# Second attention of a four-stage transformer kernel: the first scores run three slots ahead, the sixteen shifts are turned and sent together, and the visits to TensorE's whole array are regrouped

## The reference

```
x = LN(x + attention0(x))     # 16 heads of 8, rotary embedding
x = LN(x + ffn0(x))           # ternary weights, gelu, inner LN, 512 wide
x = LN(x + attention1(x))     # below
x = LN(x + ffn1(x))           # gated silu, 384 wide
```

```
h = LN(x) * ln_g + ln_b
qk, v = split(h @ W_kv)                   # one projection serves as query and as key
scores = qk[h] @ qk[h].T                  # 16 heads, 256 x 256
a1 = softmax(scores, axis=-1)
a1 = W_x mixed over heads                 # 16 x 16
o1 = a1 @ v ;  return o1 @ W_out
```

## Time and profile before

| What | Value |
|---|---|
| median of three runs | 1552.67 us |
| the profiled execution's own time | 1553.82 us |
| its span, first to last instruction | 1551.6 us |
| TensorE busy (matmuls) | 1467.2 us, 95% of the span |
| TensorE weight loads | 1145.0 us |
| VectorE busy | 1187.8 us, 77% |
| ScalarE busy | 1051.0 us, 68% |
| GpSimd busy | 966.2 us, 62% |
| mean granted TensorE clock | 0.975 of full speed |

### The profile page before, as it was taken

How to read it: one execution, slowest core, us unless ns; L and a number is a source line. 1 busy time by engine, 2 the same in 40 slices (tenths; PEclk the granted TensorE clock), 3 DMA queues, 4 the chain that set the end, 5 groups by cost and what they waited for, 6 DMA issues and landing times. The chain is left out here.

```text
span 1551.6 us, 55296 instructions
## 1 busy us (share of the span) xinstructions
PE 1467.2 (95%) x17642; PEld 1145.0 (74%) x17642; DVE 1187.8 (77%) x3338; ACT 1051.0 (68%) x2581; POOL 966.2 (62%) x1160
## 2 busy tenths in 40 slices
PE   5999999999999799979999999999999999998998
PEld 3444555554554399959888888888888888997997
DVE  4777888888888478887878888788878887864666
ACT  2466777777778788856767777777777777774332
POOL 4555565655654067777778877887788777852222
PEclk8799999999999999979999999999999999999999
DMA  5344544454454100122222222222222222200111
GB/s 144 101 131 119 136 128 134 127 136 132 131 136 117 45 32 30 43 87 76 78 72 78 80 76 76 79 80 77 73 81 80 78 70 82 77 23 28 64 64 51
DMA packets 174124, 133.93 MB, mean 86 GB/s; under 512 B 13787, under 2 KB 145126, under 8 KB 174054
## 3 DMA queue, kind: packets, MB, share of 16 engines
q1 hardware_dynamic: 172944, 132.37, 29.4%
q10 hardware_dynamic: 1110, 0.66, 0.1%
HBM read 64.82 MB, written 55.05 MB: 77 GB/s over the span
## 5 line engine op out<-in xcount | busy, mean ns | idle before, releaser
L934 DVE TENSOR_REDUCE shifts<-bank 128x2 bf16<-128x512 f32 x1024 | 684.4, 688 | 169.7 <-PE bank L1086 166.0
L879 ACT ACTIVATE probs<-bank 128x512 f32<-128x512 f32 x1024 | 573.6, 594 | 139.6 <-PE bank L1072 138.2
L1034 PE MATMUL bank<-values,probs 64*128 64x129 f32 x8192 | 579.6, 277 | 3.8 <-DVE o_even L901 0.7
L1034 PEld LDWEIGHTS bank<-values,probs 64*128 64x128 f32 x8192 | 527.1, 188 | 30.6 <-issue 10.8
L1086 PE MATMUL bank<-stack 48*128 48x256 bf16 x2048 | 367.8, 277 | 38.8 <-DMA stack<-score_parts 20.6
L1072 PE MATMUL bank<-stack 49*128 49x256 bf16 x2048 | 376.4, 274 | 8.5 <-ACT probs L879 3.1
L680 POOL TENSOR_TENSOR values<-mix,v_in 128x1024 f32<-128x1024 f32 x128 | 302.0, 2361 | 0.0
L1072 PEld LDWEIGHTS bank<-stack 49*128 49x128 bf16 x2048 | 166.1, 95 | 140.8 <-ACT probs L879 90.2
L689 POOL TENSOR_TENSOR o_odd<-o_odd,scaled 128x256 f32<-128x256 f32 x224 | 163.3, 729 | 161.4 <-ACT scaled L803 161.1
L1086 PEld LDWEIGHTS bank<-stack 48*128 48x128 bf16 x2048 | 156.4, 96 | 61.8 <-DVE shifts L934 24.4
L803 ACT ACTIVATE scaled<-bank,recips 128x128 f32<-128x128 f32 x448 | 137.6, 357 | 88.7 <-DVE recips L928 88.7
(11 more groups left out here) (165 smaller groups left out, 2179.4 us busy)
## 6 DMA issues: line engine op xcount, KB each, us to landing
stack<-score_parts SPq DMA_DIRECT2D x64, 512.0 KB, 4.0
stack<-score_parts SPq DMA_DIRECT2D x256, 96.0 KB
score_parts<-parts SPq DMA_DIRECT2D x256, 64.0 KB, 2.1
score_parts<-parts SPq DMA_DIRECT2D x128, 96.0 KB, 2.3
score_parts<-parts SPq DMA_DIRECT2D x64, 192.0 KB, 2.3
x_in_f<-x_all SPq DMA_DIRECT2D x64, 128.0 KB, 2.0
score_parts<-parts SPq DMA_DIRECT2D x64, 128.0 KB, 2.3
x_in<-in_L_attn_x SPq DMA_DIRECT2D x32, 128.0 KB, 4.3
```

Source lines behind the costliest of these rows:

```text
L879: act.activation(probs[:, s % RING, :, :].rearrange("p t n -> p (t n)"), s2[s % 2][:, :], ACT.Exp, scale=scale).then_inc(exp_done, 1)
L934: dve.tensor_reduce(shifts[:, :, hf, col], s1_bank(s)[:, :].rearrange("p (t n) -> p t n", t=TILES), op=ALU.max, axis=AX.X, negate=True).th ...
L1034: return pe.matmul(pv_bank(h)[:, q * (D + 1):(q + 1) * (D + 1)], probs[rows, h % RING, t, q * P:(q + 1) * P], values[b.odd][rows, t, h, :] ...
```

## The change

- **Lead.** First scores run `LEAD = 3` slots further ahead: slot s holds index s+3 of batch i+1, and slots 13 to 15 hold indices 0 to 2 of batch i+2. `first_score` and `max_of_head` keep `h = s ^ 1`, now of the shifted index. Step -1 does the first three indices besides its own.
- **Shifts.** All sixteen maxima of a batch go into one buffer (two buffers in turn), are turned by two transposes at slot 13, copied once, and sent by one DMA. SyncE issues it between the two halves of `stack_in`.
- **Visits.** There are three: slot 8 (transposes of `x` and `o`), slot 11 (projection of `q`, now for batch i+3, and output projection), slot 13 (projection of `v`, then all shifts).
- **Copies and splits.** ScalarE takes `exact` at slot 12, part 0 at slot 13 (from `exact` in SBUF instead of PSUM) and part 1 at slot 15. GpSimd's two subtractions move from slots 2 and 5 to 13 and 15. The two normalisations, both at slot 15 before, stand at slot 15 and slot 0.
- **Waits.** `parts_out` waits until the stack of batch i+1 has been read (before: batch i). `take_qk` waits for `y_ready` of batch i-1.

The core of the diff:

```diff
+LEAD = 3
-        self.shifts1 = 2 if first else 1
-        self.shifts0 = 10 if first else 9
+        self.shifts1 = 2 if first else None
+        self.shifts0 = 10 if first else 13
-        self.xt, self.xt_ahead = (6, 4) if first else (13, 3)
-        self.q, self.q_ahead = (14, 4) if first else (1, 2)
+        self.xt, self.xt_ahead = (6, 4) if first else (8, 3)
+        self.q, self.q_ahead = (14, 4) if first else (11, 3)
-        self.ot = 10 if first else 9
+        self.ot = 10 if first else 8
-        self.split = 3 if first else 2
+        self.split = 3
...
+    def first_scores_at(i, on, s):
+
+        if first:
+            return [(i.plus(1), s)] if on(1) else []
+        lead_in = isinstance(i.half, int) and i.number() < 0
+        if s < HEADS - LEAD:
+            scores = [(i.plus(1), s + LEAD)] if on(1) else []
+        else:
+            scores = [(i.plus(2), s + LEAD - HEADS)] if on(2) and not (lead_in and i.number() == -2) else []
+        if lead_in and i.number() == -1 and s == 0:
+            scores = [(i.plus(1), k) for k in range(LEAD)] + scores
+        return scores
...
+        def all_shift_rows_in(b):
+
+            wait_apart(sp, shift_rows_ready, b.number() + 1)
+            rows = core.stack[b.odd][SHIFT_ROW:SHIFT_ROW + TILE_ROWS + 1:TILE_ROWS, 1, :, :]
+            sp.dma_start(rows.rearrange("q r n -> q (r n)"), shift_rows[:, :]).then_inc(shifted[0], 16)
...
-                wait_apart(sp, stacked[0], times(i, 0, n) * (16 * reads))
-                wait_apart(sp, stacked[1], times(i, 0, n) * (16 * reads))
+                read = times(i, 0 if first else 1, n) * (16 * reads)
+                wait_apart(sp, stacked[0], read)
+                wait_apart(sp, stacked[1], read)
...
                 stack_in(i.plus(2), i, on, 0)
+            if not first and on(1):
+                all_shift_rows_in(i.plus(1))
+            if on(2):
                 stack_in(i.plus(2), i, on, 1)
...
-                if s == 2 and on(slots.split):
+                if s == 13 and on(slots.split):
                     split(i.plus(slots.split))
-                if s == 5 and on(slots.split):
+                if s == 15 and on(slots.split):
                     last_part(i.plus(slots.split))
...
+            wait(act, y_ready, times(b, -4, n))
             wait(act, rest_ready, times(b, -1, n))
-            act.activation(exact[:, 0, :], m1[:, 0:TOK], ACT.Copy).then_inc(qk_taken, 1)
...
+            act.activation(exact[:, 0, :], m1[:, TOK:2 * TOK], ACT.Copy).then_inc(qk_taken, 1)
+
+        def first_part(b):
+
+            wait(act, parts_written, times(b, -2, n) * (16 * writes))
+            act.wait_ge(qk_taken, times(b, 0, n))
+            act.activation(parts[b.odd][:, 0, 0, :], exact[:, 0, :], ACT.Copy).then_inc(part0_ready, 1)
...
                 if not first and s == slots.norm and on(-1):
-                    norm(i.plus(-1))
+                    norm(i.plus(-1), (0,))
+                if not first and s == (slots.norm + 1) % HEADS and on(-2):
+                    norm(i.plus(-2), (1,))
...
+        def all_shifts_turned(b):
+
+            pe.wait_ge(max_done, (b.number() + 1) * HEADS)
+            for t in range(TILES):
+                to = SHIFTS_AT + t * P
+                last = pe.transpose(m0[:, :].bitcast(BF16)[0:P, to:to + P], shifts[b.odd][:, t, :], core.ident_bf[:, :])
             last.then_inc(shifts_in_psum, 1)
...
                 if h == BESIDE:
-                    pe.wait_ge(shift_rows_ready, (b.number() + 1) * 2)
-                    pe.wait_ge(part0_ready, times(b, 2, n))
+                    pe.wait_ge(shift_rows_ready, b.number() + 1)
                     pe.wait_ge(v_taken, times(b, 1, n))
...
+            *before, ahead = first_scores_at(i, on, s) or [None]
+
             def score(row_tile, t):
                 if s % 2 == row_tile:
                     if on(0):
                         second_score(i, s, t)
-                elif on(1):
-                    first_score(i.plus(1), s, t)
...
+                elif ahead:
+                    first_score(*ahead, t)
```

More of the change, by code:

```diff
@@ L654, in step @@
                     parts_out(b)
-            if on(1):
+            if first and on(1):
                 shift_rows_in(i.plus(1), 0)
@@ L851, in step @@
                     wait(act, values_ready, times(i, 1, n) * (2 * TILES))
-                    act.activation(v_in[:, :, :].rearrange("p t d -> p (t d)"), m0[:, TOK:2 * TOK], ACT.Copy).then_inc(v_taken, 1)
+                    act.activation(v_in[:, :, :].rearrange("p t d -> p (t d)"), m0[:, 0:TOK], ACT.Copy).then_inc(v_taken, 1)
+                if not first and s == 15 and on(slots.q_ahead):
+                    second_part(i.plus(slots.q_ahead))
                 if s == 13 and first and on(0):
@@ L857, in step @@
                     act.activation(o_t[:, :], m1[:, 0:TOK], ACT.Copy).then_inc(ot_ready, 1)
-                if s == slots.shifts0 and on(1):
+                if first and s == slots.shifts0 and on(1):
                     shift_rows_out(i.plus(1), 0)
+                if not first and s == slots.shifts0 and on(1):
+                    all_shift_rows_out(i.plus(1))
                 if s == slots.xt + (1 if first else 0) and on(slots.xt_ahead):
@@ L986, in _ @@
         if not first:
-            dve.memset(shifts[:, :, :, half_heads:P], 0.0).then_inc(ones_ready, 1)
+            for k in range(2):
+                dve.memset(shifts[k][:, :, HEADS:P], 0.0).then_inc(ones_ready, 1)
         for v in values:
@@ L1213, in others_of_second @@
                     pe.wait_ge(pv_taken, (i.number() * half_heads + (BESIDE // 2 + 1)) * TILES)
-                shifts_turned(i.plus(1), 0)
+            if s == slots.xt and on(3):
+                b = i.plus(3)
+                pe.wait_ge(x_loaded[b.odd], (b.half + 1) * 16)
+                for t in range(TILES):
+                    last = pe.transpose(m1[:, TOK + t * P:TOK + (t + 1) * P], x_in[b.odd][:, t, :], core.ident[:, :])
+                last.then_inc(xt_in_psum, 1)
             if s == slots.ot and on(-1):
                 pe.wait_ge(o_ready, times(i, -1, n))
-                wait(pe, y_ready, times(i, -2, n))
-                if on(0):
-                    pe.wait_ge(pv_taken, (i.number() * half_heads + (BESIDE // 2 + 1)) * TILES)
                 for t in range(TILES):
@@ L1222, in others_of_second @@
                 last.then_inc(ot_in_psum, 1)
+            if s == slots.q and (on(slots.q_ahead) or on(-1)):
+                wait(pe, xt_ready, times(i, slots.q_ahead, n))
+                wait(pe, ot_ready, times(i, -1, n))
+            if s == slots.q and on(slots.q_ahead):
+                b = i.plus(slots.q_ahead)
+                pe.matmul(m1[:, TOK:2 * TOK], core.w1_qk[:, :], x_t[b.odd][:, :], start=True, stop=True).then_inc(qk_in_psum, 1)
             if s == slots.out and on(-1):
-                pe.wait_ge(ot_ready, times(i, -1, n))
-                if on(1):
-                    pe.wait_ge(shift_rows_ready, i.plus(1).number() * 2 + 1)
                 for t in range(TILES):
@@ L1239, in others_of_second @@
                 for t in range(TILES):
-                    last = pe.matmul(m0[:, TOK + t * P:TOK + (t + 1) * P], x_t[b.odd][:, t * P:(t + 1) * P],
+                    last = pe.matmul(m0[:, t * P:(t + 1) * P], x_t[b.odd][:, t * P:(t + 1) * P],
                                      core.w1_kv[:, 1, :], start=True, stop=True)
                 last.then_inc(v_in_psum, 1)
-            if s == slots.xt and on(3):
-                b = i.plus(3)
-                pe.wait_ge(x_loaded[b.odd], (b.half + 1) * 16)
-                for t in range(TILES):
-                    last = pe.transpose(m1[:, t * P:(t + 1) * P], x_in[b.odd][:, t, :], core.ident[:, :])
-                last.then_inc(xt_in_psum, 1)
+            if s == slots.shifts0 and on(1):
+                all_shifts_turned(i.plus(1))
         def step(i, on):
```

78 lines of the change are left out of this document (41 added, 37 removed).

## The result

The change made the kernel slower: 1569.44 us, the median of 5 runs (1562.86 to 1575.3), against 1552.67 before. The ratio is 1.0102 with a 95% interval of 1.0074 to 1.0131. The forecast was 1546. The profiled execution has a span of 1567.3 us, 15.7 more than before.

A forecast was written before the change was run, and what follows sets the result against it. TensorE's own instruction list was taken to set the pace, 22.16 us a step; +0.8 - 0.32 - 0.67 = -0.19 a step over thirty steps, -6 us, with about 1 gained at the start, gave 1546 us, range 1528 to 1572.

The forecast's parts named there:

- The start gains about 1: At the start, about 1 us gained: second batch's stack earlier, against three more maxima ahead of the first step.
- tile term: In each steady step, both scores of a slot on one row tile cost +0.8 us; bounds nothing to +3.6.
- balance: Slots 11 and 12: the tiles get equal work, without a gap after a visit, so +0.
- Rival 1: TensorE's row tiles wait for each other: 1577 us (chance 0.09, partly) or 1631 us (0.05, wholly).
- three visits: Three visits instead of four, two shift transposes instead of four: 3.13 us against 3.45, so -0.32 a step.
- the stalls: Short stalls in a step fall from 0.87 to 0.2 us as copies and normalisation are spread: -0.67.
- rival 3: Spreading does nothing; stalls come from VectorE's maxima and reciprocals and stay at 0.87: +0.48 a step, 1567 us, chance 0.10.
- the shifts come in time: From slot 13's transposes to slot 0, the shift rows' road likely takes 2.5 of 3.5 us: cost nothing, at worst +0.5.
- Rival 2: Shifts come late: slot 13's turning or slot 0's scores wait 0.6 more than allowed; +0.41 a step, 1565 us, chance 0.14.
- stack and parts: Stack halves are needed three slots (3.3 us) earlier, parts are ready before their step begins: cost 0.
- the prediction's own mark: Period of L1206's loads should be 21.97 us; the prediction is wrong if above 22.3 or below 21.5.

The follow-up runs named there:

- e1: The new kernel with a slot's first scores back on the row tile that the second scores leave free (head s instead of s ^ 1): 1538.48 us.
- e6: The new kernel with the upper products, those of the free tile, ahead of the lower ones in even slots: 1565.11 us.
- e7: The new kernel with a lead of four slots instead of three: 1565.80 us.
- e5: The new kernel with the edits of e1 and e4 together and nothing else: 1531.97 us.
- e4: The new kernel with lead-in steps -3 and -2 split at slot 11 and SyncE's next-stage loads issued ahead of step 30's: 1564.24 us.
- e3: The new kernel with each upper product one place later in the slot's list: 1588.31 us.
- e2: The kernel before with both scores of a slot on one row tile and nothing else changed: 1563.78 us.
- e8: The kernel before with ScalarE scaling head 13 ahead of the copies of q and shift rows in slot 1: 1541.64 us.

## Why the prediction was wrong

The forecast had the span 7 shorter; it got 15.7 longer. Of the 22.7 between them, 12 lie at the ends and 10.5 in the steady steps.

*Failed: "The start gains about 1".* The ends cost 5.9 + 1.2 + 2.6 + 1.5 = 11.2. I had multiplied the steady step by thirty and looked at one effect of the rest. I read no row of the lead-in and none of the hand-over to the next stage for the moved parts. What was there:
- The gain that I named, the second batch's stack coming earlier, did come: the wait of 2.37 us for it in slot 0 is gone. It bought nothing, as ScalarE's first exponential starts 5.19 us after the first second score in both kernels, behind the last normalisation of ffn0 (the feed-forward stage before), and slot 2's scores wait for it in both.
- Three more maxima lie ahead of the first second score, which comes 17.6 after the first of the first scores instead of 14.7. I named them but gave them no price. In all kernels with a lead of three or four this stretch was 17.0 to 17.8, in those without 14.7. No run took them away by themselves.
- The lead-in does x, q and v within one step, and TensorE waits 2.94 us in it (at 642.99 to 650.76), where the kernel before waits 0.81. ffn0's matmuls, from attention 0's last score to their last one, take 148.8 against 143.8. Not all of the 5.0 is the lead-in's. The granted clock was half in 538.0 to 541.5, ahead of all changed code, and in 650.6 to 654.2, right behind the waits, and full in all of this stretch of before. With the same lead-in, e1 had the full clock throughout and took 146.9; e6 and e7 had both slow stretches and took 148.8 and 148.9. The spread lead-in of e5, at the full clock but for 0.6 us, took 146.1 and that of e4, with the first slow stretch, 145.9. So spreading saves 0.8 us at the full clock, and up to 3 where the waits are followed by half clock. What sets the slow stretches off in one kernel and not in another was not found.
- SyncE's load for the next stage is queued behind the shift rows; e4 shows that this was 3.5 us (1.9 in step 30 and 1.5 after it).
- Of step 0's 1.2, 0.7 is gone in e1 (26.69 instead of 27.39), so this part is the tile term below.

The 5.9 of the start is too small, as attention 0 ended 2.0 us earlier in this execution than in before's. It ended between 529.7 and 535.1 in the executions profiled here, with no relation to the edits. From its last score to the first second score the new kernel takes 166.6 us and before 158.6. With the same lead-in e1, e3, e6 and e7 take 164.1 to 166.9, e2 and e8 with before's lead-in 159.1 and 158.6, and e4 and e5 163.7 and 164.0. So the start costs 5 to 8 us, and most of it stays in e4 and e5.

*Mis-sized: the tile term, +0.8 a step.* The direction, the layout and the size of a plain pair (2.33 forecast, 2.34 measured) were right. Against e1 the term is 1.04, by parts: slots 8 to 10 +0.23 (forecast +0.32), slots 11 and 12 +0.15 (forecast 0, "balance"), slots 13 to 7 +0.65 (forecast +0.50). Slot 12 with its visit takes 2.32 against 2.06 (0.13 of it in the visit itself, 0.89 against 0.76), and slot 7 with its visit 2.02 against 1.79. My reading is that where a visit follows, the tile that starts late has no slot behind it in which to make up for it; no run tested this, and slots 10 and 11 with their visits lose only 0.01 together. The gap in the earlier trace rows is the wait for `half_done`, as I read it: in that last step's plain slots the uppers load 0.33 to 0.34 after it was raised, the shortest distance in any trace. But to carry it over was only half right, for in the new layout a second limit holds at nearly the same time, and that 2.33 fitted 2.34 owes something to luck. Rival 1 said that the look-ahead ends. It does, after four matmuls, and e3 and e6 show both limits, each where the other is away. Its condition, a loss from 1.0 a step up, was just met. Two waiting scores were passed over in the earlier trace rows; four are not. The packing section of the Trainium skill's page TensorE: Matmul & The Clock Gate, by which matmuls stay in strict program order, would have given +3.6 by the prediction's reckoning. The start order between tiles in the earlier trace rows and the 1.04 speak against that; its direction, slower, was right.

*Right: three visits.* Their content is 2.56 (0.59, 1.08, 0.89 in the medians) against 2.53 forecast, and 2.42 in e1, where both tiles end together.

*Mostly right: the stalls.* That ScalarE's burst in slot 1 made slot 2's stall is shown by e8, which takes 0.34 of the 0.87 away. In e1 a step is 17.84 + 2.42 + 0.60 + 0.42, so 0.42 are left, not 0.2. The largest is slot 0, by the late scaling above; this was read from the trace and not tested. So stalls fell by 0.45 where the forecast had 0.67, and for the missing third rival 3's mechanism, VectorE's chain of maxima and reciprocals, is what slot 0 shows. Visits and stalls together gave -0.82 a step (22.10 to 21.28) where the forecast had -0.99.

*Right: the shifts come in time.* Rival 2 is out: the transposes waited 0.3 us in 27 steps, and nothing waits for the shift rows' DMA. *Right, with little margin: stack and parts,* as e7 shows.

Sum of the steady part: 1.04 - 0.82 = +0.22 a step instead of -0.19, and the prediction's own mark, a period above 22.3, was passed (22.34). Over 29 steps that is 6.4; the 4.5 of the first table is less, mainly because one step of before (23.75 us) holds the late stack DMA of the earlier trace rows, 1.65 more than its neighbours.

## What to carry to other kernels

When work is moved by some slots, check its parity against every resource that alternates by slot; here one index costs 31 us, and the rebuilt order with the other index and mended ends was 20 us faster than the kernel before (e5). A forecast from the steady period must be followed by a reading of the first and last step, instruction by instruction, for everything that moved, the issue queues as well: in a phase of 32 steps the ends lost more than the steps. A long wait in the new trace is a new cost only if the work behind it comes later than in the old one. Before rebuilding a step, try to move the one late instruction that the trace shows (e8).

## What the runs showed of the hardware

- Two row tiles of TensorE are filled from one list with a short look-ahead. Behind a visit a tile's next weights were loaded when the matmul four places ahead started, 0.01, 0.24 and 0.46 us after the slot's first score for places 4, 6 and 8 (e6, the new kernel, e3). In other slots loads also came later than this. Within that look-ahead a later matmul on the other tile can start first, as in the earlier trace rows.
- From the start of the last matmul that raises a semaphore to the weight load that waits for it, on the same engine, 0.33 us passed (1003.20 to 1003.53 in e6). It was never under 0.326 in 5120 such pairs of the ten traces. With a pass of 0.27 that leaves 0.06.
- TensorE's granted clock fell to half (1.2 GHz) at about 1394.8, after an idle time of 1.59 us that had ended at 1394.22, and was back at 1398.2 with the same work under way. Fourteen passes took 1.70 instead of 0.94 in it. In e4, without the wait, the same stretch was at full clock and 3.5 us shorter, so a wait of 1.6 us cost about as much again. The waits of the lead-in, 2.94 us within 8, were followed by such a stretch in the new kernel, e6 and e7, and not in e1 and e3.
